# One kernel, four edits: layer 0's first loads moved into the setup, layer 1's mixing reordered, its head norm computed per head, layer 2's two attentions in one phase

## What is computed

```python
# layer 0: attention of 16 heads over the 461 tokens of context and x, then an MLP
x = L0(ctx_2048, x, mask, ...)
# layer 1, time mixing (RWKV), 32 heads of 16
xa = ln(x, ln1_w, ln1_b);  sx = previous_token(xa) - xa
t = tanh((xa + sx * maa_x) @ maa_w1)                   # 5 branches of 32
for f in "wkvrg":                                      # five mixed inputs
    x_f = xa + sx * (maa_f + t_f @ maa_w2[f])
w = exp(-exp(time_decay + tanh(x_w @ decay_w1) @ decay_w2))
k, v, r, g = x_k @ Wk.T, x_v @ Wv.T, x_r @ Wr.T, silu(x_g @ Wg.T)
y = scan(k, v, w, r)                                   # states of 16x16 per head
y = (y - mean_head(y)) * rsqrt(var_head(y) + eps) * gn_w + gn_b   # per head of 16
x = x + (y * g) @ Wo.T                                 # then the channel mixing
# layer 2: two cross attentions (16 heads of 128, one more key), then an MLP
for i in (1, 2):
    h = ln(x, ln{i}_scale, ln{i}_offset)
    x = x + attention(h, ctx_2048, wq{i}, ..., bias_k{i}, bias_v{i}) @ wo{i} + bo{i}
x = x + mlp(ln(x))
# layer 3: grouped attention over ctx_2048, output, layer norm
```

## Time and profile before

| | us |
|---|---|
| median of 3 runs | 3610.95 (3606.99 to 3614.26) |
| the profiled execution | 3607.46 |
| its span, first to last instruction | 3604.8 |
| TensorE busy | 3107.4 (86%) |
| VectorE busy | 1935.4 (54%) |
| ScalarE busy | 1465.9 (41%) |
| GpSimd busy | 882.0 (24%) |
| mean granted TensorE clock | 0.928 of 2.4 GHz |

### The profile page before, as it was taken

How to read it: one execution, slowest core, us unless ns; L and a number is a source line. 1 busy time by engine, 2 the same in 40 slices (tenths; PEclk the granted TensorE clock), 3 DMA queues, 4 the chain that set the end, 5 groups by cost and what they waited for, 6 DMA issues and landing times. The chain is left out here.

```text
span 3604.8 us, 47979 instructions
## 1 busy us (share of the span) xinstructions
PE 3107.4 (86%) x17295; PEld 2582.1 (72%) x17295; DVE 1935.4 (54%) x3934; ACT 1465.9 (41%) x3355; POOL 882.0 (24%) x891
## 2 busy tenths in 40 slices
PE   3899779697775878999999968999999996969996
PEld 3677569454442378998999858998999986946662
DVE  1455342416875265656566647666556565137773
ACT  1444343111011144446544534445554464237770
POOL 0222310113551241114011333112201041045622
PEclk9999789898897989999999979999999997979987
DMA  3222020100000041103301124001411022021201
GB/s 84 76 61 71 19 94 1 46 12 3 0 12 35 3 139 48 50 19 120 102 26 43 51 83 132 26 26 58 132 50 51 19 78 96 1 85 46 69 3 37
DMA packets 142468, 189.70 MB, mean 53 GB/s; under 512 B 26779, under 2 KB 109596, under 8 KB 142244
## 3 DMA queue, kind: packets, MB, share of 16 engines
q1 hardware_dynamic: 129700, 150.97, 14.0%
q0 software_dynamic: 12544, 35.77, 3.2%
HBM read 167.92 MB, written 15.50 MB: 51 GB/s over the span
## 5 line engine op out<-in xcount | busy, mean ns | idle before, releaser
L63 PE MATMUL l2a<-l_arena,l_arena 128*128 128x400 f32 (+2 forms) x1856 | 650.4, 350 | 37.0 <-DVE l_arena L2520 16.7
L65 PE MATMUL l2a<-l_arena,l_arena 128*128 128x400 f32 (+2 forms) x1856 | 631.7, 340 | 0.0
L64 PE MATMUL l2a<-l_arena,l_arena 128*128 128x400 f32 (+2 forms) x1856 | 631.7, 340 | 0.0
L63 PEld LDWEIGHTS l2a<-l_arena,l_arena 128*128 128x128 f32 (+1 forms) x1856 | 351.9, 190 | 59.9 <-issue 48.9
L64 PEld LDWEIGHTS l2a<-l_arena,l_arena 128*128 128x128 f32 (+1 forms) x1856 | 353.4, 190 | 2.7
L65 PEld LDWEIGHTS l2a<-l_arena,l_arena 128*128 128x128 f32 (+1 forms) x1856 | 351.8, 190 | 1.9
L2209 PE MATMUL l2a<-l_arena,l_arena 121*128 121x384 f32 (+1 forms) x768 | 279.3, 364 | 3.2 <-DVE l_arena L2587 3.2
L2388 ACT ACTIVATE l_arena<-l2a 121x384 fp32r<-121x384 f32 (+1 forms) x208 | 99.6, 479 | 441.9 <-PE l2a L2189 441.9
L2211 PE MATMUL l2a<-l_arena,l_arena 121*128 121x384 f32 (+1 forms) x768 | 263.9, 344 | 0.0
L2210 PE MATMUL l2a<-l_arena,l_arena 121*128 121x384 f32 (+1 forms) x768 | 263.3, 343 | 0.0
L2073 POOL DMA_DIRECT2D p_dram_layer<-l_arena x128 | 62.6, 495 | 725.9 <-DVE l_arena L2587 725.9
(11 more groups left out here) (398 smaller groups left out, 6911.3 us busy)
## 6 DMA issues: line engine op xcount, KB each, us to landing
l_arena<-in_L_xattn_wq_dram SPq DMA_DIRECT2D x32, 512.0 KB, 6.0
l_arena<-in_L_xattn_wk_dram SPq DMA_DIRECT2D x32, 512.0 KB, 7.2
l_arena<-in_L_xattn_wv_dram SPq DMA_DIRECT2D x32, 512.0 KB, 3.8
l_arena<-in_L_xattn_wo_dram SPq DMA_DIRECT2D x64, 256.0 KB, 2.7
l_arena<-ctxT_hi POOLq DMA_DIRECT2D x16, 724.0 KB, 4.6
l_arena<-ctxT_lo POOLq DMA_DIRECT2D x16, 724.0 KB, 6.0
l0mlp_staged<-in_L_xattn_mlp_w_dram SPq DMA_DIRECT2D x16, 512.0 KB, 4.2
l2mlp_staged<-in_L_xattn_w_fc_dram SPq DMA_DIRECT2D x16, 512.0 KB, 4.3
```

The source lines that it names most:

```text
L63: pe.matmul(out, cut_a(a.hi), cut_b(b.hi), start=start, stop=False)
L64: pe.matmul(out, cut_a(a.hi), cut_b(b.lo), start=False, stop=False)
L65: return pe.matmul(out, cut_a(a.lo), cut_b(b.hi), start=False, stop=stop)
```

## The change

Four edits. First, batch 0's tokens and two pieces of kv_w are loaded at the head of the setup; ScalarE's queue takes the 20 parameters of the first tile; the 512 key biases come as four rows and are turned with a stride; X is loaded in layer 0 once, after the mask of batch 1 and before the stores of batch 0's ctxT. Second, the mixing's TensorE order is mix(n + 1) before project(n). Third, the variance is gathered into one row per head (32 rows for each of four tiles in one bank), rooted and inverted for a half at once, and spread again by a product. Fourth, both attentions of layer 2 are four steps of one phase; each next half is normed inside the values loop (statistics at head 2, inverse at 3 and 4, rows at 6 to 9, turning at 8 to 11, scaling at 9 to 12), the output bias goes into the copies of the output, and no half goes through DRAM.

```diff
@@ setup
+        @block.sync
+        def _(sp):
+            sp.wait_ge(hcat_padded, 1)
+            load_first_tokens(sp, k, ins, 0)
+            for t in range(2):
+                sp.dma_start(k.kv_w[t][:], ins["L0_xattn_kv_w"][t * P:(t + 1) * P, :]).then_inc(k.kv_loaded[t], 16)
+            for r in range(2):
+                sp.dma_start(state_rows[r * B:(r + 1) * B, :], ins["ctx_2048"][:, r, :]).then_inc(loaded, 16)
+            sp.wait_ge(zeroed, 1)
+            load_params(sp, (1, 2))
+
+        @block.scalar
+        def _(act):
+            act.wait_ge(zeroed, 1)
+            load_params(act, (0,))
...
+def load_first_tokens(sp, k, ins, b):
+
+    whole = 3 * T0
+    rest = S - whole
+    context = ins["ctx_2048"]
+    sp.dma_start(k.hcat[:, 0:3, :], context[b, 0:whole, :].rearrange("(t p) d -> p t d", p=T0)
+                 ).then_inc(k.tokens_loaded, 16)
+    sp.dma_start(k.hcat[0:rest, 3, :], context[b, whole:S, :]).then_inc(k.tokens_loaded, 16)
+    sp.dma_start(k.hcat[rest:rest + L, 3, :], ins["x"][b]).then_inc(k.tokens_loaded, 16)
@@ layer0_attention
-            load_tokens(0)
-            for t in range(KT):
-                if t >= 2:
-                    sp.wait_ge(w_split, 2 * (t - 1))
+            sp.dma_start(q_w[:], ins["L0_xattn_q_w"].rearrange("(k p) n -> p k n", p=P)).then_inc(q_loaded, 16)
+            for t in range(2, KT):
+                sp.wait_ge(w_split, 2 * (t - 1))
                 sp.dma_start(kv_w[t % 2][:], ins["L0_xattn_kv_w"][t * P:(t + 1) * P, :]).then_inc(kv_loaded[t], 16)
-                if t == 1:
-                    sp.dma_start(q_w[:], ins["L0_xattn_q_w"].rearrange("(k p) n -> p k n", p=P)).then_inc(q_loaded, 16)
-                    sp.dma_start(v_bias[:], ins["L0_xattn_kv_b"].partition_broadcast(P)).then_inc(weights_loaded, 16)
-                    load_mask(0)
+            sp.dma_start(v_bias[:], ins["L0_xattn_kv_b"].partition_broadcast(P)).then_inc(weights_loaded, 16)
+            load_mask(0)
             for b in range(B):
                 if b + 1 < B:
                     load_tokens(b + 1)
                     load_mask(b + 1)
+                if b == 0:
+                    sp.dma_start(k.X[:], ins["x"].rearrange("b l d -> l b d")).then_inc(x_loaded, 16)
                 sp.wait_ge(rest_done, KT * (b + 1))
@@ layer1_mixing
-            pe.wait_ge(small, 16 * 8)
+            pe.wait_ge(small, 16)
...
+            for n in range(len(BRANCHES) + 1):
+                if n < len(BRANCHES):
+                    mix(n)
+                if n:
+                    project(n - 1)
@@ layer1_output
+            for half in range(HALVES):
+                tiles.wait_free(pe, "var", half)
+                pe.wait_ge(squared, KT * (half + 1))
+                for m in range(KT):
+                    mm = pe.matmul(tiles.bank("var", half)[group(m), 0:HALF], gather_head[:],
+                                   tile_of(square, half * KT + m), start=True, stop=True)
+                mm.then_inc(tiles.filled, 1)
+            tiles.wait_out(pe, "turn")
+            for j in range(2 * KT):
+                half, m = divmod(j, KT)
+                tiles.wait_free(pe, "inv", j)
+                pe.wait_ge(inverted, half + 1)
+                pe.matmul(tiles.bank("inv", j)[:, 0:HALF], spread_head[group(m), :], inverse[group(m), half, :],
+                          start=True, stop=True).then_inc(tiles.filled, 1)
             tiles.wait_out(pe, "Wo")
-            project_tokens(pe, tiles, "out", yT, turned, KT)
+            project_tokens(pe, tiles, "out", yT, turned, KT,
+                           lambda b: pe.wait_ge(gated, KT * (b // QUAD + 1)))
...
-            for j in range(2 * KT):
-                tiles.wait_out(dve, "var", [j])
-                dve.reciprocal(tile_of(square, j), tile_of(own_key, j)).then_inc(inverted, 1)
-                dve.wait_ge(inverted, j + 1)
-                dve.tensor_tensor(tile_of(yT, j), tile_of(yT, j), tile_of(square, j), ALU.mult).then_inc(scaled, 1)
+            for half in range(HALVES):
+                tiles.wait_out(dve, "var", [half])
+                dve.reciprocal(inverse[:, half, :], deviation[:, half, :]).then_inc(inverted, 1)
+                for m in range(KT):
+                    j = half * KT + m
+                    tiles.wait_filled(dve, "inv", j)
+                    dve.tensor_tensor(tile_of(yT, j), tile_of(yT, j), tiles.bank("inv", j)[:, 0:HALF], ALU.mult
+                                      ).then_inc(tiles.emptied["d"], 1)
@@ layer2_attention
+            def load_kb(half, p):
+                if half % HALVES:
+                    return
+                if p == 0:
+                    sp.wait_ge(h_lo, KT * (half + 1))
+                s, layer = p % 2, layer_of(half)
+                cols = slice(p * PAIR2, (p + 1) * PAIR2)
+                bias_k = ins[f"L2_xattn_bias_k{layer}"].rearrange("a b h d -> (a b h d)")
+                sp.dma_start(kb[s][:, 0, :], bias_k[cols].partition_broadcast(P)).then_inc(kb_loaded[s], 16)
+                sp.dma_start(kb[s][:, 1, :], ins[f"L2_xattn_bk{layer}"][cols].partition_broadcast(P)
+                             ).then_inc(kb_loaded[s], 16)
...
+            for half in range(STEPS):
+                if half:
+                    pool.wait_ge(h_made, KT * QUAD * half)
+                for i in range(3):
+                    last = pool.memset(probs[i][:, N2 - 1:N2], 0.0)
+                last.then_inc(padded, 1)
+                load_context(QUAD * half)
...
+                    if h == 4 and half + 1 < STEPS:
+                        invert_next(half)
...
+            def turn_next(half, c):
+
+                pe.wait_ge(next_normed, QUAD * half + c + 1)
+                if c >= 2:
+                    pe.wait_ge(h_made, KT * (QUAD * half + c - 1))
+                for t in range(KT):
+                    mm = pe.transpose(ps_next[c % 2][:, t * L:(t + 1) * L], next_rows[c % 2][0:L, t * P:(t + 1) * P],
+                                      k.ident[0:L, 0:L])
+                mm.then_inc(next_turned, 1)
...
+                    if half + 1 < STEPS and 8 <= h < 8 + QUAD:
+                        turn_next(half, h - 8)
                 project(half, H2 - 1)
+                if half + 1 < STEPS:
+                    pe.wait_ge(h_made, KT * QUAD * (half + 1))
...
+            def make_h(half, c):
+
+                act.wait_ge(next_turned, QUAD * half + c + 1)
+                layer = layer_of(half + 1)
+                for t in range(KT):
+                    act.activation(hraw[:, t, c * L:(c + 1) * L], ps_next[c % 2][:, t * L:(t + 1) * L], ACT.Identity,
+                                   bias=column(k, f"L2_xattn_ln{layer}_offset", t),
+                                   scale=column(k, f"L2_xattn_ln{layer}_scale", t)).then_inc(h_made, 1)
...
+            def sum_next(half):
+
+                dve.wait_ge(turned, STEPS2 * (half + 1))
+                if half:
+                    dve.wait_ge(added, QUAD * half)
+                for c in range(QUAD):
+                    last = dve.bn_stats(next_six[0:L, c, :], k.X[:, first_batch(half + 1) + c, :])
+                last.then_inc(next_summed, 1)
+
+            def shift_next(half):
+                dve.wait_ge(next_summed, half + 1)
+                for c in range(QUAD):
+                    last = dve.bn_aggr(next_mean_var[0:L, c, :], next_six[0:L, c, :])
+                last.then_inc(next_aggregated, 1)
+                dve.wait_ge(next_aggregated, half + 1)
+                dve.tensor_scalar(next_shifted[0:L], next_mean_var[0:L, :, 1], 1e-5, None, ALU.add).then_inc(next_ready, 1)
+
+            def norm_next(half, c):
+                if c == 0:
+                    dve.wait_ge(next_inverted, half + 1)
+                if c >= 2:
+                    dve.wait_ge(next_turned, QUAD * half + c - 1)
+                dve.tensor_scalar(next_rows[c % 2][0:L], k.X[:, first_batch(half + 1) + c, :], next_mean_var[0:L, c, 0:1],
+                                  next_inverse[0:L, c:c + 1], ALU.subtract, ALU.mult).then_inc(next_normed, 1)
...
+                    if half + 1 < STEPS:
+                        if h == 2:
+                            sum_next(half)
+                        if h == 3:
+                            shift_next(half)
+                        if 6 <= h < 6 + QUAD:
+                            norm_next(half, h - 6)
@@ layer2
 def layer2(nc, k, ins, ctx):
-    for layer in (1, 2):
-        with ExitStack() as own:
-            arena = Arena(nc, own, f"l2_arena{layer}", ARENA2)
-            whole = arena.at(0, KT, B * L)
-            norm_features(nc, k, ctx, f"l2ln{layer}", whole,
-                          f"L2_xattn_ln{layer}_scale", f"L2_xattn_ln{layer}_offset", 1e-5,
-                          add_row=ins[f"L2_xattn_bo{layer}"])
-            layer2_attention(nc, k, ins, ctx, layer, arena, whole)
+    with ExitStack() as own:
+        arena = Arena(nc, own, "l2_arena", ARENA2)
+        hraw = arena.at(19376, KT, HALF)
```

(2 more changed lines are left out.)

418 lines of the change are left out of this document (224 added, 194 removed), and 2 rows, old and new, of the table PARAM_TILES.

## The result

The changed kernel takes 3506.98 us (median of four, 3499.42 to 3518.28) beside 3610.12 us of the kernel before: ratio 0.9713, 95% interval 0.9691 to 0.9735, that is 103 us less. Five executions on another occasion gave 3512.15 us beside 3611.03, ratio 0.9727 (0.9707 to 0.9746), 99 us less. The profiled execution is the slowest of the first four, 3518.28 us with a span of 3516.5. The forecast was 3511.

A forecast was written before the change was run, and what follows sets the result against it. TensorE, busy 3107.4 of 3604.8 us, was taken as the bound, with its idle and lower-clock time to win. Terms -18 - 25 - 12.5 - 44 = -99.5 us gave a median of 3511; range 3490 to 3536.

The forecast's parts named there:

- Part 1: Setup and layer 0 loads: earlier start gains 27 us, X's later load costs 9; sum -18, bounds -30 and -12.
- the bound of 20: Setup: parameters land last, at about 16 us, at the latest 20; landing after 20 would show the forecast wrong.
- rival (a): Layer 0: X uses other engines than the tokens, or its queue has room; 9 us less, 3502; chance 0.15.
- Part 2: Layer 1's mixing: reordering removes TensorE waits and slow-clock stretches; gain 25 us, bounds 18 and 28.
- Rival (c): Mixing: late copies of turned weights stop each stage, so half of the 25 us stays; 3524; chance 0.10.
- Part 3: Layer 1's output: eight reciprocals become two, with spreading products added; gain 12.5 us, bounds 9 and 16.
- the walk: Layer 1's output, step by step: variance, root, reciprocal, spread products per half; output products at 1098.5 instead of 1111.
- Part 4: Layer 2's two attentions in one phase: start 12 and seam 39 gained, 7 paid; -44 us, bounds -53 and -29.
- Seam: Between layer 2's two attentions: next key turn at 2111.9 instead of 2146.59, worth 34.7 us.
- The values loop growing by more than 5 us in a half: Layer 2: a named sign that the forecast is wrong.
- rival (b): Layer 2's seam gives back a good part, through a stalled values loop or late context and key biases; 3526; chance 0.12.
- Rival (d): TensorE falls to 1.2 GHz in a long stretch without waits, in layer 2's values or scores loop; slower; chance 0.02.

The follow-up runs named there:

- the second profile: Profile of the changed kernel run once more, unchanged, on another occasion: span 3510.3 us; median of its five executions 3512.15 us, ratio 0.9727 to the kernel before.
- tok112: Changed kernel with each load of 116 token rows made as 112 and 4 rows: 3508.09 us, ratio 0.9716 to the kernel before.
- x_late: Changed kernel with X's load issued one batch later, behind batch 2's tokens: 3502.61 us beside 3609.37 of the kernel before, ratio 0.9708.
- u_loads: Changed kernel with setup, layer 0's loads and X's load put back as before: 3518.89 us beside 3602.78 of the kernel before, ratio 0.9764.
- u_mixing: Changed kernel with layer 1's mixing put back in its old order: 3536.95 us beside 3602.78 of the kernel before, ratio 0.9809.
- reduce_late: Changed kernel with VectorE's reduction for W0 behind its splits of the next head's weights: 3497.6 us beside 3609.37 of the kernel before, ratio 0.9696.

## Why the prediction was right, and where it was not

The sum was -99.5 us. The two measurements gave -103 and -99; by the spans, the second profile has -94.5, with 3.1 us in layer 3's attention against it. The total was right partly because a term that was too large and one that was too small stood side by side.

- **Part 1, -18; measured -13.4** at the end of layer 0's attention (436.4 to 423.0). The step that failed is the landing of the parameters: forecast at 16 us, measured 21.52, beyond the bound of 20, which the forecast had named as a sign that it was wrong. I had the four engines, and 722 KB at 95 GB/s on them, but took the queue as empty once its bytes were over. The parameters' packets still come behind the tokens' on those engines, and some 3 us pass without a packet before the wait ends. The Trainium skill (DMA: Bandwidth & Descriptors, "Queues, rings and completion order") says that a semaphore's increment lands only after every earlier write of its engine; it would make any small load as late as the large one ahead of it on the same engine. tok112 agrees: with the large loads spread, the small ones are released 3.9 us sooner. But the small loads' packets, too, come last, so that their place in the queue alone would do it, and no run tells the two apart. The gain at the q products was 23.0 us instead of 27, the lower bound. The other half was right in kind and size: X's load behind SyncE's other queued loads, wait forecast 21, measured 20.98 (19.83 to 21.24 in the seven profiles with these loads), and back at 12.22 in x_late. That disposes of rival (a), and x_late and tok112 agree with what the rule of the Trainium skill that the prediction cites (DMA: Bandwidth & Descriptors, "Why a DMA increments its semaphore by 16 and not by 1") would do to both.
- **Part 2, -25; measured -26.4 in the stage, +2.0 in the scan.** Idle time went from 25.1 to 8.6 us (182.20 - 157.07 and 155.80 - 147.22), 16.5 against the forecast's 15.5 + 1.2; busy time at the lower clock from 157.07 to 147.22, 9.9 against 9.8. The start went from 9.04 to 8.00. Rival (c) is gone: no bank wait stands ahead of a stage. The 2 us in the scan are new. They aren't the mixing's order alone: u_loads has the new order and 219.0 us of scan, and u_mixing has the new loads and 219.2. Their cause is open.
- **Part 3, -12.5; measured -16.4.** Mis-sized: the spread products, priced at 1.2 GHz and about 4 us per half, took 2.07 and 2.04, and the output started 34.3 us into the stage, not 37. The order of the walk held. 16 was the upper bound, with all of them at 2.4 GHz; it was passed at the lower level, so the clock was not what the price had wrong. The walk counted passes one behind another, and these overlap. "The variance keeps its sixteen passes" is right in number, but they took 1.8 us and not 5.5; that gave nothing on the path, since the first reciprocal ended as late as forecast (26.1 us into the stage against 25.7).
- **Part 4, -44; measured -43.6** in the second profile (11.2 in the norm, 32.4 in the attention), -36.7 in the first. Start 14.5 instead of 12 (11.1 from the norm, 3.4 from the phase's beginning to the first key turn). Seam 34.7, as forecast. The first heads gave 1.3 us and not 4.3: the wait on VectorE's reduction that the forecast names is 4.97 us where it allowed some 3, and reduce_late, with 0.82, shows that nearly the whole of it was one line's place in the order. The norm in the values loops costs 6.6 us without the long step (7 forecast: about 1.5 for the transpositions and 0.8 to 1.2 for the inversion's queue in each half), and 12.4 with it, within the bound of 16. "The values loop growing by more than 5 us in a half" was named as what would make it wrong, and in three of the eight profiles with the inversion at head 4 it did in one half (82.17 us in the third half; 82.18 in u_mixing; 80.63 in the second half of x_late). It did by the mechanism of the forecast, the inversion on GpSimd, but the forecast had put it at up to 1 us a half, without asking how late VectorE's statistics can be. So rival (b) happened in part, in some executions, and cost 6 us and not 15. The sum of part 4 came out only in the profile without it.
- **Rival (d)** did not happen: in the values loops of the second and third half the clock is 1.00 and 0.96, and over the whole kernel 0.932 where it was 0.928.

## What to carry to other kernels

Before you put a wait on an engine that also feeds another, list what is queued behind it and ask how late the awaited engine can be, not how late it is on average: a small step here stood ahead of two splits that TensorE needed. Put a reduction or a norm that nobody needs yet behind the splits of the next tile, not ahead of them. When loads are moved to the front, count which DMA engines a load's row count gives it, since small loads behind a large one on four engines are as late as that one. When you price products with only 32 rows or 32 columns, look whether those of different quarters run side by side before you count them one behind another.

## What the runs showed of the hardware

- A load of 116 rows has a tail at a DMA share of 0.3 and 102 GB/s, from 10 to 17 us in the setup. Made as 112 and 4 rows the tail is gone (332 GB/s from 8 to 10, 70 from 10 to 12, then small packets at 12), and the parameters queued behind it came 3.9 us sooner.
- About 3 us pass between the last packet of the parameters (share 0.01 from 18 to 20, 0.02 from 14 to 16 in tok112) and TensorE's release at 21.52 and 17.64. In the kernel before the packets went on until 0.5 us before it. What the queues do in this time no row shows.
- Four splits of 128x400 on VectorE took 2.0 us with GpSimd idle and 4.2 us with GpSimd's splits beside them. The rows stand side by side in the trace; no run here took one of them away.
- Eight f32 passes of 400 columns in 128 rows take 2.8 us at 2.4 GHz (16 in 5.54). Eight that write different quarters of 32 rows took 0.88 at a granted clock of 1.00, and eight that read different quarters 2.04 at 0.50.
- The same 350 us stage ran 14.3 us apart in two profiles (343.2 and 357.5 us), with TensorE's idle time alike and its busy time 15.0 us apart, on work that no edit touches.
